# Attention block with three-pass fp32r matmuls: the four output tiles of a query half accumulated side by side, key tile by key tile

## The reference

```
h    = group_norm(x, 32 groups) * w + b
q,k,v = qkv_w @ h + qkv_b                       # 512 channels each
attn = softmax(q^T k / sqrt(512))               # 1024 x 1024
o    = attn @ v^T
out  = x + out_w @ o^T + out_b
```

## Time and profile before

| | us |
|---|---|
| median of 3 runs | 2242.78 (2241.51 to 2244.41) |
| the profiled execution, its time | 2240.99 |
| the profiled execution, span of the trace | 2239.2 |
| PE busy | 2089.9 (93%) |
| DVE busy | 1619.2 (72%) |
| ACT busy | 953.3 (43%) |
| POOL busy | 415.6 (19%) |
| mean granted PE clock | 0.961 |

### The profile page before, as it was taken

How to read it: one execution, slowest core, us unless ns; L and a number is a source line. 1 busy time by engine, 2 the same in 40 slices (tenths; PEclk the granted TensorE clock), 3 DMA queues, 4 the chain that set the end, 5 groups by cost and what they waited for, 6 DMA issues and landing times.

```text
span 2239.2 us, 23037 instructions
## 1 busy us (share of the span) xinstructions
PE 2089.9 (93%) x8956; PEld 1712.7 (76%) x8956; DVE 1619.2 (72%) x1949; ACT 953.3 (43%) x1179; POOL 415.6 (19%) x237
## 2 busy tenths in 40 slices
PE   8789999898998989989899898989989899898998
PEld 6668778686886868868687786878868688686886
DVE  7678677776767678676776867767777776767754
ACT  6353344434444343444433445334453444444341
POOL 2012030211302113030120302203021130211302
PEclk9899999999999999999999999999999999999999
DMA  5204122140321303213031220402214032130303
GB/s 156 77 5 78 42 43 81 16 108 1 48 77 27 98 1 48 77 29 95 1 56 68 38 86 6 96 23 44 81 20 104 1 48 76 29 95 1 48 38 48
DMA packets 88269, 118.37 MB, mean 53 GB/s; under 512 B 47824, under 2 KB 48432, under 8 KB 88160
## 3 DMA queue, kind: packets, MB, share of 16 engines
q0 software_dynamic: 19296, 35.92, 11.4%
q1 hardware_dynamic: 68864, 80.98, 11.0%
HBM read 46.78 MB, written 67.74 MB: 51 GB/s over the span
## 4 chain that ended last, share of the span: by engine, by line
PE 68%; DVE 16%; issue 6%; ACT 6%; POOL 2%; POOLq 0%; DVEq 0%
PE ring L262 23%; PE ring L263 23%; PE ring L264 23%; DVE stage L865 3%; ACT stage L510 3%; DVE r_lo L875 2%; DVE stage L846 2%; DVE run_max L858 2%; DVE r_lo L870 2%; DVE stage L881 2%; ACT r_hi L517 2%; POOL all_max L631 1%; ACT r_hi L522 1%; DVE stage L884 1%; DVE group_mv L908 1%
## 5 line engine op out<-in xcount | busy, mean ns | idle before, releaser
L262 PE MATMUL ring<-r_hi 128*128 128x512 f32 x1568 | 636.5, 406 | 128.7 <-DVE r_lo L875 120.0
L263 PE MATMUL ring<-r_lo,r_hi 128*128 128x512 f32 x1568 | 629.7, 402 | 0.0
L264 PE MATMUL ring<-r_hi,r_lo 128*128 128x512 f32 x1568 | 628.6, 401 | 0.0
L262 PEld LDWEIGHTS ring<-r_hi 128*128 128x128 f32 x1568 | 306.5, 195 | 210.7 <-DVE r_lo L875 137.5
L264 PEld LDWEIGHTS ring<-r_hi,r_lo 128*128 128x128 f32 x1568 | 306.1, 195 | 66.2
L263 PEld LDWEIGHTS ring<-r_lo,r_hi 128*128 128x128 f32 x1568 | 306.9, 196 | 63.0
L510 ACT ACTIVATE stage<-stage 128x1024 f32<-128x1024 f32 x128 | 135.5, 1058 | 450.3 <-DVE stage L865 448.5
L497 ACT ACTIVATE stage<-ring,keybias 128x512 f32<-128x512 f32 x256 | 173.0, 688 | 248.7 <-PE ring L264 248.7
L631 POOL PARTITION_ALL_REDUCE all_max<-run_max x32 | 57.2, 1787 | 943.8 <-DVE run_max L858 668.7
L846 DVE TENSOR_TENSOR stage<-stage,ring 128x512 f32<-128x512 f32 x192 | 131.5, 685 | 115.4 <-PE ring L264 62.6
L262 PE MATMUL ring<-h_hi,g_hi 128*128 128x512 f32 x512 | 199.4, 389 | 0.0
(11 more groups left out here) (100 smaller groups left out, 3012.5 us busy)
## 6 DMA issues: line engine op xcount, KB each, us to landing
xs<-x_in SPq DMA_DIRECT2D x64, 512.0 KB, 6.0
out<-xs SPq DMA_DIRECT2D x64, 512.0 KB, 3.2
out<-run_max POOLq DMA_DIRECT2D x86, 256.0 KB, 4.3
out<-spare POOLq DMA_DIRECT2D x42, 256.0 KB, 4.5
inv<-inv_row SPq DMA_DIRECT2D x32, 256.0 KB, 3.8
stage<-stage POOLq DMA_DIRECT2D x3, 512.0 KB, 8.5
stage<-wk SPq DMA_DIRECT2D x4, 256.0 KB, 4.0
stage<-wq SPq DMA_DIRECT2D x4, 256.0 KB, 5.1
```

The source lines that it names most:

```text
L262: nc.tensor.matmul(ps_out, st_hi, m_hi, start=first, stop=False, skip_group_check=goes_on)
L263: nc.tensor.matmul(ps_out, st_hi, m_lo, start=False, stop=False, skip_group_check=goes_on)
L264: return nc.tensor.matmul(ps_out, st_lo, m_hi, start=False, stop=last, skip_group_check=goes_on)
```

## The change

Within a query half the loops are exchanged: for each key tile m, all four output tiles c are advanced by one step, each in its own bank, as before. Tile c's last step (m = 7) counts `s_unit`. The wait for V tile m, and for the exponentials, comes once for each m, ahead of c = 0. At m = 0 of the first half each c also waits until `v_rest(c)` has read the bank it is about to overwrite. The second half of the last batch element keeps the old order. The number of matmuls, their operands and the banks are the same; nothing on the other engines' queues is moved.

```diff
--- before.py
+++ after.py
@@ -386,19 +386,25 @@
                     a.then_inc(s_unit, 1)
 
             def output_units(b, nb):
-                for c in range(CT):
+
+
+                by_keys = (b, nb) != (B - 1, NB - 1)
+                steps = [(c, m) for m in range(MT) for c in range(CT)]
+                if not by_keys:
+                    steps.sort()
+                for c, m in steps:
                     cs = slice(c * P, (c + 1) * P)
-                    pe.wait_ge(s_vlo, b * 8 + CT * nb + c + 1)
-                    for m in range(MT):
-                        if c == 0:
-                            if nb == 0:
-                                pe.wait_ge(s_vlo, b * 8 + m + 1)
-                            pe.wait_ge(s_plo, b * 8 + nb * CT + m // 2 + 1)
-                        a = three(ring[:, CT * nb + c, :], v_part(v_hi_all, m)[:, cs], v_part(v_lo_all, m)[:, cs],
-                                  p_tiles(r_hi, nb, m)[:, 0, :], p_tiles(r_lo, nb, m)[:, 0, :], m == 0, m == MT - 1)
-                    a.then_inc(s_unit, 1)
-
-            v_hi_all, v_lo_all = r_hi, r_lo
+                    if m == 0 and (c == 0 or nb == 0):
+
+                        pe.wait_ge(s_vlo, b * 8 + CT * nb + c + 1)
+                    if c == 0:
+                        pe.wait_ge(s_vlo, b * 8 + m + 1)
+                        pe.wait_ge(s_plo, b * 8 + nb * CT + m // 2 + 1)
+                    a = three(ring[:, CT * nb + c, :], v_part(r_hi, m)[:, cs], v_part(r_lo, m)[:, cs],
+                              p_tiles(r_hi, nb, m)[:, 0, :], p_tiles(r_lo, nb, m)[:, 0, :], m == 0, m == MT - 1)
+                    if m == MT - 1:
+                        a.then_inc(s_unit, 1)
+
             for b in range(B):
                 t_units(b)
                 score_products(b)
```

## The result

The changed kernel takes 2094.71 us (median of 4 runs, 2092.37 to 2096.33) against 2242.15 us before: a ratio of 0.9342, with a 95% interval from 0.9326 to 0.9359. The forecast was 2096.0 us, in a range of 2068 to 2126. The profiled execution took 2092.37 us, with a span of 2090.6.

The account below looks back on a forecast made before the run. PE was taken to be bound by waits for late V tiles in O and the low clock after them. 15 x (11.33 - 2.0) + 6.5 = 146.4 us gained gave 2096 us, range 2068 to 2126.

Parts of the forecast that it names:

- What bounds the kernel before: O stage: PE waits for late V tiles and the low clock after them lose 11.33 us each, 169.9 us in 15.
- O without waits, 43.52 us: O stage: both waits and the low clock vanish, so 192 matmuls take 43.52 us in place of 54.85.
- The bank change at nothing: O stage: changing bank every 3 matmuls was taken to cost zero, as S and V run at full pace.
- The upper end of 9.7 us per stage: O stage: if each step must drain before the next bank, 0.16 us for each of 60 additional changes.
- the rival that was slower: O stage: bank changes every third matmul break PE's flow and keep the clock at 0.50, about 2670 us; chance 0.03.
- The scalings of tiles that end together at nothing: `scale_output` on DVE: tiles finish 9 and 8 us before their scalings, so DVE's queue keeps its times; cost nothing.
- What is late next: T stage and first products: PE arrives earlier, DVE does not; PE waits 2.0 us per batch element, bounds 0 and 4.
- The end: Last batch element: PE ends 8.2 us earlier, but the last scaling waits for a transfer holding its buffer; gain 6.5 us.
- The clock at full: T stage: waits come in pieces of 0.4 to 1.2 us, far shorter than 4.63, so the clock stays at full.

Follow-up runs that it names:

- e8: The changed kernel with two of the four `h_combined_rest` made twice on DVE for each batch element but the first: 2129.45 us, ratio 0.9496.
- e4: The changed kernel with output tiles 0 and 1 advanced side by side, key tile by key tile, then tiles 2 and 3: 2147.69 us, ratio 0.9587.
- e5: The changed kernel with all four `h_rest` on DVE ahead of the first `scale_output`: 2071.75 us, ratio 0.9238.

## Why the prediction was right

The sum of the terms was 146.4 us; the medians differ by 147.4, the profiled executions by 148.6. The terms came out one by one, and not by errors that cancel: 15 x 1.92 us of waits for 15 x 2.0, and 7.0 us at the end for 6.5; 0.5 us ahead of the first V stage were in no term.

- *What bounds the kernel before.* Two waits for V tiles and the low clock after them, 11.33 us in each O stage. Shown: early V tiles alone remove all of it (2063.66 us), with no change of order. That the two waits hang together, and do not each have a price of their own, is shown by the kernel with tile 5 alone early.
- *O without waits, 43.52 us.* Measured 43.52 in each of 15.
- *The bank change at nothing.* Measured, also at one for each matmul. The upper end of 9.7 us per stage and the rival that was slower fall with it. (The text counted 60 more changes of bank in a stage; it is 64 in place of 8, so 56 and 9.1 us, which changes nothing.) The Trainium skill's rule on cycling through PSUM banks (TensorE: Matmul & The Clock Gate, "A second HAM failure mode: psum-queue depth-cycling") does not show in the kernels that fill four banks side by side: 1.00 is the granted clock of their O stages. The short pauses of PE that the page speaks of do not occur there (43.52 us busy in 43.52), so these runs cannot tell what such pauses would do. In the O, T and S stages of all kernels here, each fall of the clock follows an idle time of PE.
- *The scalings of tiles that end together at nothing.* Right: DVE's chain kept its times, to 0.3 us in the example and 0.03 on average. The early V tiles give the same time in either order.
- *What is late next.* 2.0 us of waits in T for each batch element were forecast, 1.92 measured, at the three places named: up to 0.5 us at bank 7 (forecast 0.5), about 1.1 at the first product (1.1) and 0.35 at the second (0.4). That DVE's backlog is the cause is shown from both sides: 3 us less of it (early V tiles) took the waits away, 1.4 less (the h rests ahead) took 20.7 of 28.8 us, and 2.5 more added 2.5 to each T and S.
- *The end.* 6.5 us forecast, 7.0 measured: the transfer that holds the buffer was issued at 2080.68 and let the last scaling go at 2084.74, 4.1 us and not 5.1.
- *The clock at full.* Right for the changed kernel, where PE's longest wait in T and S is 0.84 us, but with less room than the text gave it. It set pieces of up to 1.2 us against a wait of 4.63 as if the way between were safe. The runs show the clock falling in 7 of 15 cases after two waits of 1.2 to 1.7 and 2.9 us, and in 10 of 15 after one of 1.77 to 2.37. Where between 0.84 and 1.77 us a single wait begins to cost the clock is not shown.

The change is not the best answer to its own wait. It gives PE other work while V tiles 5 to 7 are late, although they could be ready almost as O starts: PE has finished them 5.4, 2.7 and 0 us ahead of O. In the example, where O starts at 1089.72, ACT then stood idle from 1087.3 to 1099.0 and DVE from 1089.1 to 1092.8.

## What to carry to other kernels

Where an engine waits for tiles that come one by one, exchanging loops so that each tile opens more work hides the lateness; price it by setting the time at which each tile is wanted in the new order beside the time at which it is ready. Then replay the queue of the engine that feeds the next stage from the new, earlier start: 11.3 us saved here turned into 9.4, and that part could be read from the trace beforehand. Look first whether the late tile is only behind other work in its engine's queue: moving it ahead gave 178 us where the exchange gave 147.

## What the runs showed of the hardware that was not expected

- The granted clock of PE fell to 1.2 GHz after single idle times of 1.77 to 2.37 us in ten stretches (e8), and did not after 1.43 to 2.09 us in the other five. It fell after waits of 1.51 and 2.87 us close to each other (e4), but not after 1.00 and 2.85 us. The lengths alone do not decide: in e4 it fell in 7 of 15 O stages, with first waits of 1.17 to 1.67 us, and stayed up in 8 with 0.90 to 1.29.
- A lower clock under a bound elsewhere is nearly free: where DVE's chain held PE (e8), stretches with the fall took 0.4 us more on average than those without. In e4, where nothing else held PE after the fall, they took 1.3 us more at the least (49.6 against 48.3).
- A two-input operation of DVE that starts while POOL's all-reduce runs can be held until it ends: in e5 one 128x1024 rest of each four took 3.27 us and ended 0.09 us after the all-reduce, in 15 of 15 batch elements, against 1.21 for the others; the rest that had started 0.2 us before the all-reduce took 1.2.
